# Bias as 32 rows of the slot products instead of a ones product, and chunk 0's first two stationary blocks in transfers of their own

## The reference, cut to what matters

```python
c    = x @ W.T + b + SCALING * (x @ A[slot]) @ Bm[slot]     # slot = itok[request], 32 slots
base = c @ W_base.T + b_base
w    = top-2 of softmax over (c @ W_router.T)               # zero for the six experts not taken
lora = sum over experts of ((c @ A_e.T) * w_e) @ B_e.T * SCALING
out  = x + base + lora
```

## Time and profile before

| | us |
|---|---|
| runs | 66.47, 67.10, 67.25 |
| median | 67.10 |
| the profiled execution's own time | 67.11 |
| its span, first to last instruction | 65.3 |
| TensorE busy | 61.7 (95%) |
| VectorE busy | 36.9 (56%) |
| ScalarE busy | 22.9 (35%) |
| GpSimd busy | 17.3 (26%) |

### The profile page before, as it was taken

How to read it: one execution, slowest core, us unless ns; L and a number is a source line. 1 busy time by engine, 2 the same in 40 slices (tenths; PEclk the granted TensorE clock), 3 DMA queues, 4 the chain that set the end, 5 groups by cost and what they waited for, 6 DMA issues and landing times.

```text
span 65.3 us, 1174 instructions
## 1 busy us (share of the span) xinstructions
PE 61.7 (95%) x422; PEld 60.9 (93%) x422; DVE 36.9 (56%) x105; ACT 22.9 (35%) x46; POOL 17.3 (26%) x29
## 2 busy tenths in 40 slices
PE   5999999999999999999999999999999999999930
PEld 5979999999999999998999999999999999999920
DVE  0066579999799867115825576002768354857320
ACT  0667368707799989136103100020201040020000
POOL 6700000000699997787380000010100000000000
PEclk9999999999999999999999999999999999999999
DMA  0899998401899304245568998400044000023632
GB/s 0 226 360 346 410 407 249 113 3 53 233 319 386 139 6 102 60 105 129 125 128 306 393 394 324 177 6 0 0 161 161 10 0 0 0 80 123 217 134 88
DMA packets 6025, 10.57 MB, mean 162 GB/s; under 512 B 755, under 2 KB 2547, under 8 KB 6020
## 3 DMA queue, kind: packets, MB, share of 16 engines
q1 hardware_dynamic: 5730, 10.17, 46.5%
q10 hardware_dynamic: 290, 0.33, 1.5%
HBM read 7.37 MB, written 2.10 MB: 145 GB/s over the span
## 4 chain that ended last, share of the span: by engine, by line
PE 90%; ACT 3%; ACTq 2%; DVE 1%; issue 0%
PE ps L693 26%; PE ps L601 24%; PE ps L705 19%; PE ps L753 9%; PE ps L662 5%; PE ps L728 2%; ACT L352 2%; PE ps L733 2%; PE ps L739 1%; PE ps L716 1%; ACTq L355 1%; ACTq L356 1%; ACT wt_hi L352 1%; DVE xn L554 1%; PE ps L672 0%
## 5 line engine op out<-in xcount | busy, mean ns | idle before, releaser
L693 PE MATMUL ps<-am,x_hi 128*128 128x384 f32 x64 | 16.6, 340 | 0.0
L705 PE MATMUL ps<-bm,x_hi 128*128 128x280 f32 x64 | 13.0, 297 | 0.0
L693 PEld LDWEIGHTS ps<-am,x_hi 128*128 128x128 f32 x64 | 11.4, 188 | 0.0
L693 PE MATMUL ps<-am,x_lo 128*128 128x384 f32 x32 | 10.8, 338 | 0.0
L319 POOL TENSOR_TENSOR x_lo<-xt,x_hi 128x512 fp32r<-128x512 f32 x8 | 10.8, 1367 | 0.0
L705 PEld LDWEIGHTS ps<-bm,x_hi 128*128 128x128 f32 x64 | 10.1, 188 | 0.0
L705 PE MATMUL ps<-bm,x_lo 128*128 128x280 f32 x32 | 9.3, 290 | 0.0
L601 PE MATMUL ps<-wt_hi 128*128 128x280 f32 (+1 forms) x32 | 7.6, 335 | 0.1
L554 DVE TENSOR_TENSOR xn<-ps,xn 128x280 f32<-128x280 f32 (+1 forms) x16 | 6.1, 418 | 2.7 <-PE ps L753 2.6
L601 PE MATMUL ps<-wt_lo,wt_hi 128*128 128x280 f32 (+1 forms) x32 | 7.3, 326 | 0.0
L326 POOL CAST am<-as_hl 128x128 fp32r<-128x128 f32 x8 | 3.1, 393 | 14.2 <-PE ps L693 14.1
(11 more groups left out here) (74 smaller groups left out, 99.4 us busy)
## 6 DMA issues: line engine op xcount, KB each, us to landing
xt<-x_t SPq DMA_DIRECT2D x4, 512.0 KB, 6.1
xn<-x_n SPq DMA_DIRECT2D x4, 512.0 KB, 4.8
out_n<-xn SPq DMA_DIRECT2D x7, 256.0 KB, 2.1
wt<-w_chunks SPq DMA_DIRECT2D x2, 582.0 KB, 6.6
g_st<-g_hl SPq DMA_DIRECT2D x12, 81.0 KB, 2.1
ab<-adapters SPq DMA_DIRECT2D x8, 64.0 KB, 2.6
wt<-w_chunks SPq DMA_DIRECT2D x1, 326.0 KB, 4.6
wt<-w_chunks SPq DMA_DIRECT2D x2, 128.0 KB, 3.0
```

The source lines that it names most:

```text
L693: last = mm(a_bank(b)[:, 0:R + WA], v[:, p, i, tok], am[:, i, level, at:at + R + WA], start=(i == 0 and n == 0), stop=False, skip_group_ch ...
L705: mm(b_bank(b)[:, 0:QB], v[:, p, i, tok], bm[:, i, level, :], start=(i == 0 and n == 0), stop=False, skip_group_check=True)
```

## The change

Two parts. In the first, the ones product goes. `bsum`, folded to 64 rows as before, is folded twice more: VectorE adds rows 32 to 63 and `b_base` (which now arrives as 32 rows, the first of them full and the others zero) into `upper`, and `upper` onto rows 0 to 31. These two additions stand in the block loop ahead of block 2. SP then copies rows 16 to 31 to partitions 0 to 15 (`moved`), VectorE adds them onto rows 0 to 15 (`folded`), ahead of the low parts of the slot products. ACT and VectorE split the 16 rows, and SP spreads 16 high and 16 low rows over the four pairs in two transfers. `g_st` and `h_t` have 128 rows instead of 100. The two matmuls of line 672, the ones tile and its rounding on GpSimd, the split of `bsum_st`, the split of `b_base`'s row and its two transfers are gone. `routed(0)` now waits for six low parts at its start and for all eight only ahead of its block 3. `stack_transpose(1)` no longer waits for the bias.

In the second part, blocks 2 and 3 of chunk 0 arrive in two transfers of 128 columns instead of one of 256, each with its own semaphore, so that ACT rounds block 2 without waiting for block 3; and the slot numbers are issued by SP, fourth in its queue, not by ACT. Besides, ACT rounds `x` of pairs 2 and 3 in two instructions each instead of one.

```diff
+QP = HP // 2
+NC = (P - 6 * R) // 2
-W0_PIECES = [slice(D // 2, D), slice(0, D // 2), slice(D, D + QB), slice(D + QB, CB)]
+W0_PIECES = [slice(2 * P, 3 * P), slice(3 * P, D), slice(0, 2 * P), slice(D, D + QB), slice(D + QB, CB)]
-GK = CROW + 4
+GK = CROW + 2 * NC
...
         @block.sync
-            for n in (0, 1):
+            for n in (0, 1, 2):
                 sp.dma_start(wt[:, 0, W0_PIECES[n]], w[:, 0, W0_PIECES[n]]).then_inc(w0_in[n], 16)
+            sp.dma_start(idx_sb[:], idx).then_inc(idx_in, 16)
...
-            sp.dma_start(bb, bbase).then_inc(bbase_in, 16)
+            sp.dma_start(bb[QP:HP], bbase).then_inc(bbase_in, 16)
...
-            sp.wait_ge(bb_hi_done, 1)
-            spread(CROW, bb_hl[:, 0:1, :])
-            sp.wait_ge(bb_lo_done, 1)
-            spread(CROW + 1, bb_hl[:, 1:2, :])
+            sp.wait_ge(quarter_done, 2)
+            sp.dma_start(moved, bsum[NC:QP]).then_inc(moved_in, 16)
...
-                    sp.wait_ge(c_hi_done, 2)
-                    sp.wait_ge(c_lo_done, 2)
-                    for i in range(2):
-                        spread(CROW + 2 + i, c_hl[:, i:i + 1, :])
+                    for i, ready in enumerate((c_hi_done, c_lo_done)):
+                        sp.wait_ge(ready, 1)
+                        sp.dma_start(g_st[CROW + i * NC:CROW + (i + 1) * NC, :, :].bitcast(F32),
+                                     c_hl[:, i:i + 1, :].bitcast(F32).to_broadcast([NC, PAIRS, WC])
+                                     ).then_inc(cst_in, 16)
...
         @block.gpsimd
-            nc.gpsimd.memset(ones[:], 1.0).then_inc(const, 1)
-            pool.wait_ge(const, 1)
-            nc.gpsimd.tensor_copy(ones_r[:], ones[:]).then_inc(ones_rounded, 1)
...
         @block.scalar
-            for n in (2, 3):
+            for n in (3, 4):
                 act.dma_start(wt[:, 0, W0_PIECES[n]], w[:, 0, W0_PIECES[n]]).then_inc(w0_in[n], 16)
-            act.dma_start(idx_sb[:], idx).then_inc(idx_in, 16)
-            act.wait_ge(w0_in[0], 16)
             for i in (2, 3):
+                act.wait_ge(w0_in[i - 2], 16)
...
-                step = 2 if p < 2 else KB
-                for k in range(0, KB, step):
+                for k in range(0, KB, 2):
...
-                if i == 1:
-                    act.wait_ge(halves_done, 1)
-                    hi(bsum_st[0:HP], bsum[0:HP]).then_inc(bsum_hi_done, 1)
-            act.wait_ge(bbase_in, 16)
-            hi(bb_hl[:, 0], bb).then_inc(bb_hi_done, 1)
-            act.wait_ge(c_done, 1)
-            for s, c in enumerate(COLS):
-                hi(c_hl[0:1, 0, c], ps[0:1, C_BANK + s, 0:c.stop - c.start]).then_inc(c_hi_done, 1)
+            act.wait_ge(folded, 1)
+            hi(c_hl[:, 0], bsum[0:NC]).then_inc(c_hi_done, 1)
...
         @block.vector
-                if i == 1:
-                    dve.wait_ge(bsum_hi_done, 1)
-                    lo(bsum_st[HP:P], bsum[0:HP], bsum_st[0:HP]).then_inc(bsum_lo_done, 1)
+                if i == 2:
+                    dve.wait_ge(bbase_in, 16)
+                    dve.wait_ge(halves_done, 1)
+                    nc.vector.tensor_tensor(upper[0:QP], bsum[QP:HP], bb[QP:HP], ALU.add).then_inc(quarter_done, 1)
+                    dve.wait_ge(quarter_done, 1)
+                    nc.vector.tensor_tensor(bsum[0:QP], bsum[0:QP], upper[0:QP], ALU.add).then_inc(quarter_done, 1)
...
-            dve.wait_ge(bb_hi_done, 1)
-            lo(bb_hl[:, 1], bb, bb_hl[:, 0]).then_inc(bb_lo_done, 1)
+            dve.wait_ge(moved_in, 16)
+            nc.vector.tensor_tensor(bsum[0:NC], bsum[0:NC], moved, ALU.add).then_inc(folded, 1)
...
-            for s, c in enumerate(COLS):
-                dve.wait_ge(c_hi_done, s + 1)
-                lo(c_hl[0:1, 1, c], ps[0:1, C_BANK + s, 0:c.stop - c.start],
-                   c_hl[0:1, 0, c]).then_inc(c_lo_done, 1)
+            dve.wait_ge(c_hi_done, 1)
+            lo(c_hl[:, 1], bsum[0:NC], c_hl[:, 0]).then_inc(c_lo_done, 1)
...
         @block.tensor
-            pe.wait_ge(ones_rounded, 1)
-            pe.wait_ge(bsum_hi_done, 1)
-            pe.wait_ge(bsum_lo_done, 1)
-            pe.wait_ge(m_lo_done, 4)
-            for s, c in enumerate(COLS):
-                last = mm(ps[:, C_BANK + s, 0:c.stop - c.start], ones_r[:], bsum_st[:, c], start=True, stop=True)
-            last.then_inc(c_done, 1)
...
                 if b == 0:
-                    pe.wait_ge(m_lo_done, 2 * KB)
+                    pe.wait_ge(m_lo_done, 2 * (KB - 1))
...
+                    if b == 0 and i == KB - 1:
+                        pe.wait_ge(m_lo_done, 2 * KB)
...
-                if p == 1:
-                    pe.wait_ge(c_lo_done, 2)
...
-                    pe.wait_ge(cst_in, 64)
+                    pe.wait_ge(cst_in, 32)
```

More of the change, by code:

```diff
@@ L100, in build @@
         bsum = sb("bsum", [P, WC])
-        bsum_st = sb("bsum_st", [P, WC], F32R)
-        cb_hl = sb("cb_hl", [HP + 1, 2, WC], F32R)
-        c_hl, bb_hl = cb_hl[0:1], cb_hl[HP:HP + 1]
+        bb = sb("bb", [HP, WC])
+        c_hl = sb("c_hl", [NC, 2, WC], F32R)
         h_stack = sb("h_stack", [P, PAIRS, 2 * HSTEP])
@@ L115, in build @@
         hw_flat = hw[:].rearrange("p a t c -> p (a t c)")
-        upper, bb = hw_flat[0:HP, 0:WC], hw_flat[HP:HP + 1, 0:WC]
+        upper, moved = hw_flat[0:HP, 0:WC], hw_flat[0:NC, 0:WC]
         hw_hi = sb("hw_hi", [P, NB, P], F32R)
@@ L120, in build @@
         ident = sb("ident", [P, P])
-        ones = sb("ones", [P, P])
-        ones_r = sb("ones_r", [P, P], F32R)
         iota = sb("iota", [P, NE])
         ps = ctx.enter_context(nc.psum_tensor("ps", [P, 8, 512], F32))
-        G_BANK, C_BANK = 0, 2
+        G_BANK = 0
         def first_bank(p):
@@ L138, in x_rounded @@
         def x_rounded(p, n):
-            return 2 * p + n + 1 if p < 2 else 3 + p
+            return 2 * p + n + 1
         def rt_at(b):
@@ L198, in build @@
         halves_done = sem("halves_done")
-        bsum_hi_done = sem("bsum_hi_done")
-        bsum_lo_done = sem("bsum_lo_done")
+        quarter_done = sem("quarter_done")
+        moved_in = sem("moved_in")
+        folded = sem("folded")
         g_done = sem("g_done")
@@ L255, in _ @@
                 sp.dma_start(xt[:, p], x[:, p]).then_inc(x_in[p], 16)
-            def spread(row, src):
-                sp.dma_start(g_st[row:row + 1, :, :].bitcast(F32),
-                             src.bitcast(F32).to_broadcast([1, PAIRS, WC])).then_inc(cst_in, 16)
-            sp.wait_ge(bb_hi_done, 1)
-            spread(CROW, bb_hl[:, 0:1, :])
-            sp.wait_ge(bb_lo_done, 1)
-            spread(CROW + 1, bb_hl[:, 1:2, :])
+            sp.wait_ge(quarter_done, 2)
+            sp.dma_start(moved, bsum[NC:QP]).then_inc(moved_in, 16)
             for p in range(PAIRS):
@@ L352, in hi @@
                 return nc.scalar.activation(dst, src, ACT.Copy)
-            for n in (2, 3):
+            for n in (3, 4):
                 act.dma_start(wt[:, 0, W0_PIECES[n]], w[:, 0, W0_PIECES[n]]).then_inc(w0_in[n], 16)
-            act.dma_start(idx_sb[:], idx).then_inc(idx_in, 16)
-            act.wait_ge(w0_in[0], 16)
             for i in (2, 3):
+                act.wait_ge(w0_in[i - 2], 16)
                 c = slice(i * P, (i + 1) * P)
                 hi(wt_hi[:, 0, c], wt[:, 0, c]).then_inc(w0_hi_done, 1)
+            act.wait_ge(w0_in[4], 16)
+            hi(wt_hi[:, 0, D + QB:CH], wt[:, 0, D + QB:CH]).then_inc(wc_hi_done, 1)
             act.wait_ge(w0_in[3], 16)
-            hi(wt_hi[:, 0, D + QB:CH], wt[:, 0, D + QB:CH]).then_inc(wc_hi_done, 1)
-            act.wait_ge(w0_in[2], 16)
             nc.scalar.activation(bsum[:], wt[:, 0, D:CH], ACT.Copy,
@@ L374, in x_high @@
                 act.wait_ge(x_in[p], 16)
-                step = 2 if p < 2 else KB
-                for k in range(0, KB, step):
-                    hi(x_hi[:, p, k:k + step, :], xt[:, p, k:k + step, :]).then_inc(x_hi_done, 1)
+                for k in range(0, KB, 2):
+                    hi(x_hi[:, p, k:k + 2, :], xt[:, p, k:k + 2, :]).then_inc(x_hi_done, 1)
             w_high(1)
@@ L446, in _ @@
             b0 = slice(D, D + QB)
-            dve.wait_ge(w0_in[2], 16)
+            dve.wait_ge(w0_in[3], 16)
             nc.vector.tensor_copy(wt_hi[:, 0, b0], wt[:, 0, b0]).then_inc(b0_hi_done, 1)
@@ L450, in _ @@
             lo(wt_lo[:, 0, b0], wt[:, 0, b0], wt_hi[:, 0, b0]).then_inc(wc_lo_done, 1)
-            dve.wait_ge(w0_in[1], 16)
+            dve.wait_ge(w0_in[2], 16)
             nc.vector.tensor_copy(wt_hi[:, 0, 0:D // 2], wt[:, 0, 0:D // 2]).then_inc(w0_first_done, 1)
@@ L504, in stack @@
                 if p == 0:
-                    dve.wait_ge(const, 5)
+                    dve.wait_ge(const, 4)
                 nc.vector.tensor_copy(
@@ L710, in stack_transpose @@
                 if p == 0:
-                    pe.wait_ge(const, 2)
-                if p == 1:
-                    pe.wait_ge(c_lo_done, 2)
+                    pe.wait_ge(const, 1)
```

(3 more changed lines are left out.)

4 lines of the change are left out of this document (removed).

## The result

The changed kernel takes 71.94 us in the median of six runs (70.78 to 72.49). The kernel before took 66.71 beside it (66.44 to 67.25, six runs). The ratio is 1.0625, with a 95% interval of 1.056 to 1.069: slower by 6%. 67.9 was predicted, with a range of 66.5 to 68.4. "Slower by over 2%" had a chance of 0.12. Both the number and the answer were wrong.

The account below looks back on a forecast made before the run. TensorE, busy for 95% of the span, was taken as the bound; removed matmuls count fully, new waits their length. Net waits +0.45 (−0.30 contained) and +0.35, start 0: 67.11 + 0.8 + 0 = 67.9 us, range 66.5 to 68.4.

Parts of the forecast that it names:

- The two matmuls, −0.30: Two ones matmuls ahead of `routed(0)`, all on TensorE's path, go: −0.30 us.
- The bias rows "leave SP behind 28.1 and land 2.1 later": Ahead of `slots_routed(0)`: rows land at 30.2, needed at about 30.5, so hidden with 0.3 us of cover.
- The start, "I take 0 and hold −0.1 to +0.15": First blocks of chunk 0: an earlier start gains TensorE at most 0.14 us; taken as 0, held −0.1 to +0.15.
- rival 3: Start: block 3 and blocks 0 and 1 late, TensorE pauses, full speed 1.4 us later: 68.6 us; chance 0.08.
- block 3 could be late: Start: one issue of 0.43 us further back in SP's queue, block 3 can be up to 0.3 us late.
- the advice of the Trainium skill to coalesce transfers under 64 KB: Start, split transfers of 64 KB each: by that rule block 3 is late and the start loses its 0.15.
- The adapters as late as 15.8: SP's queue: adapters move from 14.88 to as late as 15.8; 0.64 us covered, up to 0.25 would shift GpSimd.
- rival 2: Adapters land at 16 or later, GpSimd starts 0.3 late, `routed(0)` waits 0.3 us for `x`: 67.2 us; chance 0.08.
- The additions and GpSimd's halves: VectorE's additions and GpSimd's halves of `x` exclude each other: TensorE waits 0.75 at `routed(0)`, 0.35 at `stack_transpose(0)`; net +0.8 us.
- the low parts of the slot products: At `routed(2)`: needed at 27.6, there at 26.5, so hidden.
- rival 1: First addition goes ahead of the half of `x`, only the second waits (1.0): 66.8 us; chance 0.26.

Follow-up runs that it names:

- part 1: Kernel before with only the bias as 32 rows (and ACT's rounding of `x` in two instructions), start as before: 71.29 us, ratio 1.061.
- The run with 22 constants: Kernel before with 22 instead of 28 constant matmuls ahead of TensorE's first real one: 68.63 us, ratio 1.030.
- part 2 alone: Kernel before with only three transfers for chunk 0's blocks and the slot numbers issued by SP: 68.02 us, 66.78 to 69.29.
- The run with the split alone: Kernel before with only the first stationary blocks' transfer split in two, indices still issued by ACT: 67.39 us, ratio 1.013.
- the run with pair 0's rows first: Bias as 32 rows with the start of before; pair 0's bias rows in own transfers, the others behind pair 1's rows: 66.97 us, ratio 1.003.
- with them filled: Kernel before with the changed start, plus ten constant products ahead of the waits for block 3 and blocks 0 and 1: 67.30 us, ratio 1.010.

## Why the prediction was wrong, point by point

**The two matmuls, −0.30: right.** `routed(0)` moved by 1.57 where the start had moved by 1.87.

**The bias rows "leave SP behind 28.1 and land 2.1 later": the step that failed.** They left at 27.9 and 28.6, close to that although the start was late. The last landed at 33.56, 4.9 us behind its issue. The 2.1 was the earlier trace rows, copies of 81 KB to 32 partitions; the new ones are 162 KB each, two in flight together, to 16 partitions. Twice the bytes, half the partitions and two at once in flight: none of the three entered the price, and I wrote "0.3 of cover" under it with no upper bound. An estimate from the rows: the two together carry 332,000 bytes, at 102 GB/s 3.3 us of transfer; what a lone one of them takes besides is 3.5 − 1.6 = 1.9. That makes 5.2 of the 5.6 us from the first issue (27.93) to the last landing; pair 1's rows, issued behind them, share the engines. The term, the landing of the last, was mis-sized by 2.8 us. In the run that makes only these transfers small 4.3 of the 4.5 us of part 1 go.

**What a pause costs behind itself: left out.** I priced waits at their length. Behind this one the clock fell to 1.2 GHz, and the chain paid 0.35 + 1.31 us more in the profiled run. The two fastest runs, with the full clock, are 1.7 us faster than the profiled one, which is the same amount; another run with the lower mean clock is only 0.7 slower than they are, so the start varies as well.

**The start, "I take 0 and hold −0.1 to +0.15": wrong, and what happened is rival 3's.** TensorE paused 0.45 us for block 3 and 0.12 for blocks 0 and 1, the rise came at about 9.8 instead of 5.88, and G began 1.87 late. The prediction had priced it with 1.4 us more at half speed; it was 3.9. I had given it 0.08, against it that TensorE is "as busy as now" before and after the pause. The run with 22 constants shows that the rise can come later with no transfer changed; whether the pause or the missing work makes it late stays open, and other profiles have such pauses and an early rise. I had also said that block 3 could be late; that blocks 0 and 1, one issue further back, come late too was only in the rival. Their cast began at 5.16 in the profile after, behind a wait for the transfer. For this step the size varies by the run: 0 to 2.5 us in part 2 alone. Beside the sum the prediction had set the advice of the Trainium skill to coalesce transfers under 64 KB (DMA: Bandwidth & Descriptors, "Rules for kernel authors"), at a loss of 0.15; the pieces are 64 KB each, at that bound and not under it. The run with the split alone lost 0.6 (67.39 against 66.83). It pointed the right way; that the overhead of small transfers is the reason isn't shown, since each piece behind the first also leaves one issue later.

**The adapters as late as 15.8: not so.** In the profile after ACT's rounding of the adapters, which waits for them, begins at 13.8 (14.88 before), and GpSimd's `as_hl` is late (17.51 against 16.91) because VectorE is. So rival 2 falls.

**The additions and GpSimd's halves: right in kind, smaller.** In the profile after, the first lasts 1.48 (0.65 behind a half of `x`), the second 0.82 because GpSimd happened to wait for ACT. TensorE was late by itself and waited for neither. With the start of before it waited 0.5 at `routed(0)`, where the prediction had 0.75, and not at `stack_transpose(0)` but at `routed(2)`, for the copy that the same exclusion holds. For `routed(2)` the prediction had looked only at the low parts of the slot products (needed at 27.6, there at 26.5) and not at this copy. Net of the 0.30 the forecast for this was +0.8 and the run with pair 0's rows first gives +0.2 (interval −0.1 to +0.5). The phase was rival 1's, which had −0.3 to −0.1 for it; the truth lies between the two.

## What to carry to other kernels

Price a transfer by its bytes over the partitions that it touches on its narrower side, and add up what is in flight with it (the copy of rows 16 to 31 took 2.1 us alone and 6.0 beside the loads of `x`): a duration from a row with other partitions and another size is one end of a range and not the price. When a product waits for a transfer, send first only the part that it reads, here one pair of four. And a pause of TensorE can cost more than its length: the clock fell behind the waits of 2.4 and 2.9 us, and with pauses in the start the runs spread up to 2.6 us. Splitting a first transfer to start earlier is worth nothing if the next piece then leaves one issue later and opens such a pause.

## What the runs showed of the hardware that was not expected

- 162 KB from SBUF to SBUF land in 3.5, 2.6 or 2.1 us by the partitions touched (16 neighbours, 16 eight apart, 128; the last with rows half as long). Neighbours on either side alone are as slow as on both, to 0.2 us.
- 40.5 KB to 16 neighbouring partitions land in 2.1 us when the DMA engines are busy for a tenth of the time (21 to 24 us with pair 0's rows first), and in 5.5 to 6.0 beside transfers of 512 KB.
- At the start the pace is half while the profile's granted clock reads 1.00 in every slice: loads for 280 columns 0.23 us apart, later 0.13. The pace in the timeline tells it, the granted clock doesn't. Behind the long pause in the middle, the granted clock does fall to 0.50 and agrees with the pace.
- The moment of the rise differs with nothing in the start changed (5.88 before, about 5.0 and 6.5 in two kernels with the same start). With part 2's pauses the spread of the runs grows from 1.0 to 2.5 us, and with them filled it is 0.6.
- Six constant products less, 0.67 us of work that computes nothing, cost 1.9 us. Why, the longer pause or the missing work, isn't shown.
